# First attention: row maxima one step further ahead of the scores, and kept in two sets

## The reference, cut to what matters

```python
def _L0_attn_ref(x, ...):
    kv_c = x @ W_kv
    kv_c = kv_c * rsqrt(mean(kv_c * kv_c) + EPS) * g_kv
    q_c = x @ W_q
    k_content, v, q_content = heads(kv_c @ W_kdec), heads(kv_c @ W_vdec), heads(q_c @ W_qdec)
    k_rope, q_rope = rope(heads(x @ W_krope)), rope(heads(q_c @ W_qrope))
    q, k = concat([q_content, q_rope]), concat([k_content, k_rope])
    scores = where(causal, einsum('bhqd,bhkd->bhqk', q, k) * scale, -inf)
    attn = softmax(scores, axis=-1)
    out = einsum('bhqk,bhkd->bhqd', attn, v)
    return out.transpose(0, 2, 1, 3).reshape(B, T, H * D) @ W_o

x = x + _L0_attn_ref(_layernorm(x), ...)
x = x + _L0_ffn_ref(_layernorm(x), ...)
x = x + _L1_attn_ref(_layernorm(x), ...)
x = x + _L1_ffn_ref(_layernorm(x), ...)
```

## Time and profile before

| | us |
|---|---|
| median of 3 runs | 1501.66 (1500.64 to 1509.76) |
| the profiled execution | 1515.03 |
| its span, first to last instruction | 1513.2 |
| PE busy in the span | 1247.5 |
| DVE busy | 1114.4 |
| ACT busy | 815.7 |
| POOL busy | 685.6 |
| pair 28: its first score product to that of pair 29 | 730.77 to 750.65 |

### The profile page before, as it was taken

One profiled execution on the slowest core, in us unless ns is written; L12 is line 12 of the kernel. 1 busy time (PEld: TensorE's weight loads), 2 busy tenths in 40 slices (PEclk: granted clock), 3 DMA queues, 4 the chain that ended last, 5 costly groups with the idle time before them and its releaser, 6 DMA issues.

```text
span 1513.2 us, 40070 instructions
## 1 busy us (share of the span) xinstructions
PE 1247.5 (82%) x14676; PEld 892.7 (59%) x14676; DVE 1114.4 (74%) x3616; ACT 815.7 (54%) x1971; POOL 685.6 (45%) x1042
## 2 busy tenths in 40 slices
PE   4499889988899988999988899589989998647780
PEld 2255545555455554555556899467777777547660
DVE  5588687886878868888665665558788878755666
ACT  1155555555555555555555455178787657326663
POOL 3023241233432334323223654466666768674664
PEclk9699999999999999999999899777887757668995
DMA  5656727556275572755741311022111112222335
GB/s 120 108 96 91 115 29 117 87 92 107 30 121 81 91 115 28 119 81 91 119 181 35 102 47 30 25 69 63 46 45 44 35 34 76 99 68 81 89 85 173
DMA packets 73892, 123.37 MB, mean 82 GB/s; under 512 B 17534, under 2 KB 46083, under 8 KB 72800
## 3 DMA queue, kind: packets, MB, share of 16 engines
q1 hardware_dynamic: 63896, 104.97, 36.6%
q0 software_dynamic: 7616, 13.59, 2.8%
q10 hardware_dynamic: 2184, 2.25, 0.8%
HBM read 30.40 MB, written 17.60 MB: 32 GB/s over the span
## 4 chain that ended last, share of the span: by engine, by line
PE 43%; DVE 28%; POOL 9%; ACT 8%; issue 6%; DMA 3%; ACTq 1%; DVEq 1%; SPq 0%; POOLq 0%
DVE first L843 7%; PE A L640 6%; DVE S L846 4%; PE S L1099 4%; PE S L611 4%; PE S L622 4%; PE S L1659 3%; DVE tA L822 3%; POOL xq L1468 2%; PE A L1670 2%; PE A L1106 2%; DMA Qp<-mT 2%; DVE tB L823 2%; PE S L1645 2%; PE S L1676 2%
## 5 line engine op out<-in xcount | busy, mean ns | idle before, releaser
L727 ACT ACTIVATE P<-S 128x512 f32<-128x512 f32 (+3 forms) x768 | 330.6, 491 | 285.6 <-PE S L622 283.3
L622 PE MATMUL S<-Qp,Kp 121*128 121x512 f32 (+3 forms) x768 | 258.2, 394 | 39.1 <-DMA Qp<-mT 11.8
L907 POOL TENSOR_SCALAR_AFFINE_SELECT P<-P 128x256 f32<-128x256 f32 x256 | 112.6, 443 | 373.8 <-ACT P L727 373.1
L846 DVE CUSTOM_DVE_ANT_0 S<-S,later 128x512 f32<-128x512 f32 (+3 forms) x512 | 238.9, 514 | 53.7 <-PE S L611 52.4
L611 PE MATMUL S<-Kp,Qp 120*128 120x512 f32 (+3 forms) x768 | 243.4, 389 | 30.7 <-DMA Kp<-big 16.3
L622 PEld LDWEIGHTS S<-Qp,Kp 121*128 121x128 f32 x768 | 137.4, 190 | 123.9 <-DVE first L843 24.6
L843 DVE TENSOR_REDUCE first<-S 128x1 f32<-128x512 f32 x256 | 164.3, 682 | 55.0 <-PE S L611 54.5
L611 PEld LDWEIGHTS S<-Kp,Qp 120*128 120x128 f32 x768 | 132.9, 194 | 112.5 <-issue 49.7
L640 PE MATMUL A<-P,V 128*9 128x256 f32 (+1 forms) x2816 | 174.5, 343 | 5.4 <-POOL P L907 4.6
L640 PEld LDWEIGHTS A<-P,V 128*9 128x9 f32 x2816 | 63.9, 90 | 70.9 <-issue 29.8
L1896 POOL TENSOR_TENSOR prod<-mid,kT 128x128 f32<-128x128 f32 x160 | 68.0, 459 | 72.1 <-ACT mid L1727 45.4
(11 more groups left out here) (358 smaller groups left out, 2585.7 us busy)
## 6 DMA issues: line engine op xcount, KB each, us to landing
Qp<-big SPq DMA_DIRECT2D x63, 256.0 KB
Kp<-big SPq DMA_DIRECT2D x62, 256.0 KB
Qp<-big SPq DMA_DIRECT2D x63, 128.0 KB
Kp<-big SPq DMA_DIRECT2D x62, 128.0 KB
xq<-xq SPq DMA_DIRECT2D x71, 72.0 KB
yb<-yq SPq DMA_DIRECT2D x8, 528.0 KB, 7.2
big<-in_w SPq DMA_DIRECT2D x4, 1024.0 KB, 9.9
big<-vt SPq DMA_DIRECT2D x32, 128.0 KB
```

The source lines that it names most:

```text
L622: te.matmul(S[s][:, 512 * h + c:512 * h + 512], K[0:121, h, 128 * kb:128 * kb + 128], Q[0:121, h, 512 * qh + c:512 * qh + 512], start=True ...
L727: se.activation(k.P[(w.n - 1) % NP0][:, h, c:512], S[s][:, 512 * h + c:512 * h + 512], ACT.Exp, scale=SCALE0).then_inc(p.done("st").h, 1)
L846: ins = ve.tensor_tensor_reduce(out=of, in0=of, in1=k.later[:, 512 - n:512], scale=1.0, scalar=-3e38, op0=ALU.add, op1=ALU.max, accum_out= ...
L907: ge.affine_select(P[:, :, c:c + 128], P[:, :, c:c + 128], [[0, 2], [1, 128]], ALU.is_ge, 0.0, base=0, channel_multiplier=-1).then_inc(p.s ...
```

## The change

`EARLY` becomes 4; `mx` and `first` become two sets, picked by the pair's parity; DVE's wait is for `mxT` of two pairs before; and in the list `mxT` of a pair stands behind piece 0 of the next pair, not ahead of it. Step s of pair u now does piece s+4 of pair u+1 up to s = 7, and steps 8 to 11 do pieces 0 to 3 of pair u+2, with `mxT` of pair u+1 behind piece 0 at step 8. No instruction is added or taken away.

```diff
-EARLY = 3
+EARLY = 4
...
-        self.mx, self.first, self.mT = sb("mx", [128, 2, 8]), sb("first", [128, 2, 4]), sb("mT", [16, 128], F32R)
+        self.mx, self.first, self.mT = [sb(f"mx{i}", [128, 2, 8]) for i in range(2)], [sb(f"firsts{i}", [128, 2, 4]) for i in range(2)], sb("mT", [16, 128], F32R)
...
         def maxima(u, i):
 
+            if u < NU:
+                o.add("mx", u, *pieces[i], ring="S")
             if i == 0 and u > 0:
                 o.add("mxT", u - 1, ring="S")
-            if u < NU:
-                o.add("mx", u, *pieces[i], ring="S")
...
-            if u:
-                dve.wait_ge(p.made("mxT"), u)
-            n = 128 * (qt + 1) - 512 * part
+            if u > 1:
+                dve.wait_ge(p.made("mxT"), u - 1)
+            n, mx = 128 * (qt + 1) - 512 * part, k.mx[u % 2]
```

More of the change, by code:

```diff
@@ L614, in attn0_tensor @@
             pe.wait_ge(p.done("mx"), 24 * w.n)
-            te.transpose(S[s][0:16, 0:128], k.mx[:].rearrange("p h n -> p (h n)"), p.ident[:]).then_inc(p.made("mxT").h, 1)
+            te.transpose(S[s][0:16, 0:128], k.mx[w.at[0] % 2][:].rearrange("p h n -> p (h n)"), p.ident[:]).then_inc(p.made("mxT").h, 1)
         elif w.kind == "st":
@@ L842, in attn0_vector @@
                 if part == 0 and qt >= 4:
-                    ve.tensor_reduce(k.first[:, h, qt - 4:qt - 3], S[s][:, 512 * h:512 * h + 512], AX.X, ALU.max).then_inc(p.done("mx").h, 1)
+                    ve.tensor_reduce(k.first[u % 2][:, h, qt - 4:qt - 3], S[s][:, 512 * h:512 * h + 512], AX.X, ALU.max).then_inc(p.done("mx").h, 1)
                     continue
@@ L846, in attn0_vector @@
                 ins = ve.tensor_tensor_reduce(out=of, in0=of, in1=k.later[:, 512 - n:512], scale=1.0, scalar=-3e38, op0=ALU.add, op1=ALU.max,
-                                              accum_out=k.mx[:, h, qt:qt + 1])
+                                              accum_out=mx[:, h, qt:qt + 1])
                 if qt == 0 and h == 1:
                     dve.then(ins)
-                    ins = ve.tensor_tensor(k.mx[:, :, 4:8], k.mx[:, :, 4:8], k.first[:], ALU.max)
+                    ins = ve.tensor_tensor(mx[:, :, 4:8], mx[:, :, 4:8], k.first[u % 2][:], ALU.max)
                 ins.then_inc(p.done("mx").h, 1)
```

## The result

| | before | after |
|---|---|---|
| median, us | 1501.15 (1498.44 to 1509.76, 4 runs) | 1532.15 (1527.84 to 1536.94, 4 runs) |
| the profiled execution, us | 1515.03 | 1527.84 |
| its span, us | 1513.2 | 1525.9 |
| first score product starts, us | 77.35 | 82.02 |
| last score product ends, us | 802.74 | 825.15 |

The changed kernel is slower: ratio 1.0188, 95% interval 1.0150 to 1.0226. In the two traces the first attention ends 22.4 us later. The rest of the program, which the change doesn't touch, took 710.5 us in the profiled execution of before and 694 to 701 in the nine other traces of this study; so the spans differ by only 12.7, and the end of the attention is the better measure of the change. What the medians show beyond 22.4 can't be placed: only profiled runs leave a trace.

What follows compares the result with a forecast made beforehand. A hand-over between PE (43% of the chain) and DVE (28%) was taken as the bound. Terms summed to 20.6 us gained; two thirds, 14 us, gave 1501 against 1515.03 profiled, 1487.7 against the median; range 1469 to 1508.

Steps and rivals of the forecast that it cites:

- seven quiet pairs: Pairs without rotary work or a load wait: four gain 1.4 us each, 15, 23 and 30 gain 1.0; 8.6 us.
- pairs 0, 8, 16, 24: Quiet in their first eight steps only: 1.0 us gained each, 4 us together.
- pairs 4g-2, for K of pair 4g: Pairs 2, 6, ... 26: piece 0 of pair 4g moves to step 8 and waits for K; -1 us, from -6 to +6.
- pairs 4g-3, rotary, with the row: Rotary pairs: 4 us gained from DVE's wait for POOL's `low`, 3 us from PE's wait for the row.
- norm and projection pairs: Pairs 3, 11, 19 and 4, 12, 20: turn now ahead of an eight-block transpose; 0.8 us a pair, 5 us gained.
- start: Ahead of pair 0's scores the turn stands behind piece 0 of pair 1, which waits for K: 3 us lost.
- The odd steps: Quiet pairs: pieces 1, 3, 5, 7, 9, 11 at odd steps, behind P times V; 1.4 us less per pair.
- PE decided before and does after: Quiet pair, step 7 to 9, piece 11 for piece 10: PE sets the length, turn added, 2.70 to 2.75 us.
- No gain worth a number: The row's DMA in quiet pairs: turn earlier on PE but `mT` behind piece 0 on DVE; no gain, none lost.
- Its own rule: Pairs 4g-2: time from K's last issue to piece 0 before, less K's landing time (3.3 us) and 1.85 more work.
- the slower rival: K stops PE at step 8 of pairs 4g-2 and the clock falls behind it: +17 us, 1519; chance 0.12.
- the signs that the prediction named for being wrong: Quiet pairs as long as before; waits for K over 2.5 us; or rotary pairs longer by more than 1 us.

Runs made afterwards that it cites:

- work in place of the stop: Changed kernel with eight unread 512-column products on PE ahead of its wait for K of pairs 4, 8, ... 28: 1519.85 us, ratio 1.0103.
- mending the join: Changed kernel with the join of first and mx (L850) behind piece 9, not piece 11: 1520.67 us, ratio 1.0103.
- mending K: Changed kernel with piece 0 of pair 4g at step 9 again in pairs 4g-2, step 8 having the turn alone: 1518.21 us, ratio 1.0052.
- both with the start put back: Changed kernel with join behind piece 9, piece 0 of pair 4g at step 9, first turn ahead of piece 0 of pair 1: 1506.27 us, ratio 0.9995.

## Why the prediction was wrong

Forecast and measured change by the terms of the sum. Measured is the difference of the two traces, pair by pair, which adds up, but for rounding, to the 22.4 us by which the attention ends later (pair 31 is the same in both):

| term | forecast, us | measured, us |
|---|---|---|
| seven quiet pairs (7, 15, 23, 27 to 30) | -8.6 | -11.5 (138.3 to 126.7) |
| pairs 0, 8, 16, 24 | -4 | -1.4 |
| pairs 4g-2, for K of pair 4g | +1 | +22.0 (141.0 to 163.0) |
| pairs 4g-3, rotary, with the row | -7 | +9.3 (191.8 to 201.1) |
| norm and projection pairs | -5 | -0.6 |
| start | +3 | +4.7 |
| sum | -20.6 | +22.4 |

*The odd steps* were right in four of five stretches: 3.2, 2.6, 3.1 and 5.2 were forecast for 9 to 11, 11 to 1, 1 to 3 and 3 to 7, and 3.23, 2.59, 3.04 and 5.43 came. But 7 to 9 took 3.31 for 2.75: "PE decided before and does after" failed, since the score now waits for ACT's exponentials (1.09 in the chain above). That one stretch takes back 0.6, and with 5.43 for 5.2 an undisturbed quiet pair gains 0.65 us (18.25 to 17.60), not 1.4. That the seven quiet pairs still gave 11.5 for the 8.6 forecast is luck. Seven times 0.65 is 4.6; nearly all the rest is the row, for which the prediction had "No gain worth a number". PE's waits from the first score of pair 27 to the end of the attention, before and after:

```profile
PE S L622 <- DMA Qp<-mT: 4.7, 3, 2.8
```

```profile
PE S L622 <- DMA Qp<-mT: 0.9, 1, 0.9
```

Ahead of pairs 16 and 24 another 1.7 and 1.3 us of such waits are gone. `mT` ends 4.3 us ahead of the next pair's first score in pairs 27 and 28, where 3.6 was forecast.

*Pairs 4g-2* is the step that failed most: "So K lands at most 3.9 us behind its last issue ... I take 3.3." It lands about 4.0 behind. The 3.9 bounded pair 6 alone; by the semaphore events K came 4.05 behind in pair 10 of before, and up to 4.16 in the others. In pair 10 that turned a stop of 1.1 us into 2.11. The sum also had nothing in it for the clock, and too little for the work behind K. The seven pairs reach piece 0 of pair 4g 5.7 us sooner in all and take 27.7 longer from there to the next pair's first score, where the prediction had seven times 1.85, 13.0; with work in place of the stop, and so at full clock, it is 16.6. Its own rule, put to the seven distances of before (3.93 to 5.34), gives -2.1 and not -1 with K at 3.3, and -7 with K at 4.0. What makes up the 3.6 us between 13.0 and 16.6 stays open.

K's time and the clock were in the slower rival, with 3.9 as its price for K and anything later than 3.5 as the point from which it decides. I gave it 0.12 because 3.9 was an upper bound and because "the clock fell behind a longer stop". The second reason was a misreading: of the row's 4.53 us PE stood for 1.59, no longer than most of the stops that the sum itself had for K (1.1 to 2.5). On PE, before:

```profile
750.65 0.87 PE L622 MATMUL S<-Qp,Kp 121*128 121x512 f32 x2 [1.59 <-DMA Qp<-mT]
```

The rival's 1.0 a stop for the clock was near the mean (9 us over seven stops, by the run with work in place of the stop, 1.3 each), the whole a pair too low, 1.9 for 3.1 (22.0 over seven). The waits for the row that it added in quiet pairs didn't come, so its 1519 was on the right side partly for another reason. What I should have read: 3.93 us from the last issue to piece 0 without a wait, in the tightest of the seven pairs, is no slack. K's last recorded event stood 0.14 us ahead of it, and the only other transfer that I had looked at took 4.53.

*Rotary pairs* is the other: I counted DVE's pieces around `rope` and overlooked the join, 0.17 us long, which the new order puts 0.16 us behind the start of `low`. No rival had it. The trace of before had the sign of it: the join took 0.68 in the rotary pairs and 0.17 elsewhere. The forecast gain of 7 didn't come either: with the join moved these pairs still take 2.4 us more than before. The 3 of it for the row had nothing to take from: none of before's eight waits for the row stands at the end of a pair 4g-3. Of the 4 for `low`, DVE's wait fell by 2.7 us (10.6 to 7.9), which doesn't show in the pairs' time.

*Norm and projection pairs* hardly gained: the turn's wait of 2.0 us is gone, and what took its place I didn't follow. *The start* was right in kind: the turn stood behind piece 0, and `mT` ended 3.0 us later, as forecast; but the first score came at 82.02, forecast near 80, since from the end of `mT` to the score it was 5.0 us, for 3.4 before. The same order began at 80.9 to 81.5 in the four other traces that have it, and at 77.35 to 81.29 in the four that have one set and the turn ahead, so how much of the 4.7 us is the change's can't be said from one trace of each. The rows before the first scores, which answer to the earlier trace rows:

```profile
74.74 1.19 PE L611 MATMUL S<-Kp,Qp 120*128 120x512 f32 x2 [3.32 <-DMA Kp<-big]
75.73 0.41 PE L615 MATMUL S<-ident,mx 128*16 128x128 f32 x1
...
82.02 1.22 PE L622 MATMUL S<-Qp,Kp 121*128 121x512 f32 x2 [3.52 <-DMA Qp<-mT]
```

Of the signs that the prediction named for being wrong, two came: a wait for K over 2.5 us (3.1), and rotary pairs longer by more than 1 us. The runs that undo one loss each agree with the table: mending the join gives the attention back 5.7 us, mending K 12.0, and both with the start put back 25.5. What stays open is why pairs 4g-3 of the mended kernels take some 2 us more than before's, and how much of the start is the order's. Of the former, 0.8 in pairs 1 and 9 stands also in the kernel before with only its join moved (27.37 and 27.30), so it need not be the fourth step's. The range's low end was also added up wrongly: the whole sum and the upper bounds named for it give 29.6 us, 1472, not 1469.

## What to carry to other kernels

Before you do a piece of work a step earlier, ask of everything that it reads when that arrives: a wait of zero in the trace says that it was there in time, not by how much, and the shortest distance seen without a wait is the value to plan with, not a bound to shave. Look also at what a moved instruction of a sixth of a microsecond will stand beside; next to a long POOL operation it can take the whole of that operation's time. And price a stop of PE with the clock behind it.

## What the hardware showed that I had not expected

A DVE `tensor_tensor` of 128x8 took 2.23 us in place of 0.17 beside a POOL `tensor_tensor`, ending as that did (711.14 and 711.12). The Trainium skill, "SBUF — State Buffer", section "Who interferes with whom", says that a DVE instruction with two SBUF inputs contends with a GpSimd instruction that reads SBUF, and calls the port pair that they share an exclusive lock; the trace agrees. The reductions, whose scores come from PSUM, keep their length beside `low`: with the join at piece 9, two plain ones took 1.29 us in all while it ran (704.96, in `low` from 703.90 to 706.25), and 1.27 after it in the rows above.

After a stop of 2.11 us the clock stayed at 0.50 for 12 us in which PE was busy throughout (2.00 of 2.00 in each window); after the stop of 1.83 in pair 26 it was back two windows later:

```profile
734.00:736.00 2.00, 1.85 (x14) 0.67 (x18) 0.58 (x2) 1.35 (x3) 0.97 (x2) 0.66 1.01 121
736.00:738.00 2.00, 2.00 (x12) 1.05 (x5) 0.41 (x1) 0.00 (x0) 0.00 (x1) 0.50 0.53 129
738.00:740.00 2.00, 1.72 (x13) 1.29 (x12) 2.00 (x6) 0.66 (x2) 0.41 (x1) 0.99 0.99 119
```

All seven stops of the changed kernel were followed by the 0.50 level; with the join moved it was six of seven (not the stop of 2.30 in pair 14), and before, the longest wait for the row, 2.83 us ahead of pair 30, was followed by none. So the price of a stop varies from nothing to several us, and what decides it wasn't tried.
